# Five fetch buffers and a later place for two tiles' corner fetches in a four-layer convolution kernel

## The reference

```python
def _bilinear_sample_one(img, px, py):
    x0 = jnp.floor(px)
    y0 = jnp.floor(py)
    x1 = x0 + 1.0
    y1 = y0 + 1.0
    wx1 = px - x0
    wx0 = 1.0 - wx1
    wy1 = py - y0
    wy0 = 1.0 - wy1
    ...
    return tap(x0, y0, wx0 * wy0) + tap(x1, y0, wx1 * wy0) + tap(x0, y1, wx0 * wy1) + tap(x1, y1, wx1 * wy1)
...
x = x + _L0_conv_ref(_gn(x), L0_conv_Wg, L0_conv_bg, L0_conv_Wexp, L0_conv_bexp)
x = x + _L1_conv_ref(_gn(x), L1_conv_w_route, L1_conv_b_route, L1_conv_w_experts)
x = x + _L2_conv_ref(_gn(x), L2_conv_codebook)
x = x + _L3_conv_ref(_gn(x), L3_conv_w_grid, L3_conv_b_grid, L3_conv_w_conv)
return x
```

## Time and profile before

| what | value |
|---|---|
| median of three runs | 1796.74 us |
| the profiled execution | 1798.24 us |
| its span, first to last instruction | 1796.4 us |
| PE busy | 1571.3 us (87%) |
| DVE busy | 1501.9 us (84%) |
| POOL busy | 1220.5 us (68%) |
| ACT busy | 1105.4 us (62%) |

### The profile page before, as it was taken

One profiled execution on the slowest core, in us unless ns is written; L12 is line 12 of the kernel. 1 busy time (PEld: TensorE's weight loads), 2 busy tenths in 40 slices (PEclk: granted clock), 3 DMA queues, 4 the chain that ended last, 5 costly groups with the idle time before them and its releaser, 6 DMA issues.

```text
span 1796.4 us, 41875 instructions
## 1 busy us (share of the span) xinstructions
PE 1571.3 (87%) x15564; PEld 1294.5 (72%) x15564; DVE 1501.9 (84%) x2927; ACT 1105.4 (62%) x1547; POOL 1220.5 (68%) x1437
## 2 busy tenths in 40 slices
PE   4686689899998989889899899989998898988998
PEld 3545666688667876588667796678865797668998
DVE  5486589888998988878798788988899778987998
ACT  2021666477655866467665686648765676658996
POOL 6143467767778667685677867776777866778774
PEclk9898799999999999989998999999999999999999
DMA  7476965697768975599656997679776895335653
GB/s 163 118 174 133 212 193 165 178 238 215 195 177 199 237 207 162 158 225 209 195 161 166 242 218 196 172 191 240 221 194 165 211 224 166 84 90 162 164 155 86
DMA packets 280768, 326.09 MB, mean 182 GB/s; under 512 B 205572, under 2 KB 219924, under 8 KB 276720
## 3 DMA queue, kind: packets, MB, share of 16 engines
q1 hardware_dynamic: 235768, 226.01, 47.9%
q0 software_dynamic: 37040, 82.95, 19.7%
q10 hardware_dynamic: 7760, 14.45, 2.5%
HBM read 253.50 MB, written 56.40 MB: 173 GB/s over the span
## 4 chain that ended last, share of the span: by engine, by line
PE 38%; DVE 19%; DMA 13%; issue 8%; DVEq 7%; POOL 7%; SPq 5%; ACT 2%; ACTq 1%; POOLq 0%
PE bank L1444 22%; DMA words<-in_codebook,code 7%; DVE code L1311 5%; DVEq L1310 4%; POOL fetched L665 3%; PE bank L1526 3%; PE bank L1558 3%; POOL words L712 3%; SPq L472 2%; PE bank L1575 2%; DMA y_patches<-yc 2%; DVE strip L1078 2%; DVE samp L1098 2%; PE bank L1424 2%; DMA arena<-xp 1%
## 5 line engine op out<-in xcount | busy, mean ns | idle before, releaser
L665 POOL DMA_INDIRECT fetched<-row_pairs,corner x768 | 735.5, 958 | 360.6 <-issue 198.0
L1444 PE MATMUL bank<-lent,tent 128*128 128x160 f32 x6144 | 935.8, 307 | 16.9 <-ACT lent L845 11.6
L1444 PEld LDWEIGHTS bank<-lent,tent 128*128 128x128 f32 x6144 | 870.5, 195 | 104.0 <-issue 71.0
L831 ACT ACTIVATE tent<-lent,row_at_sb 128x768 f32<-128x768 f32 x512 | 448.9, 924 | 56.0 <-PE bank L1444 38.9
L835 ACT ACTIVATE tent<-tent 128x1536 f32<-128x1536 f32 x256 | 379.9, 1484 | 20.9 <-issue 0.4
L1078 DVE TENSOR_TENSOR strip<-bank,near 128x480 f32<-128x480 f32 x512 | 331.1, 648 | 67.2 <-PE bank L1444 61.1
L712 POOL DMA_INDIRECT words<-in_codebook,code x256 | 246.4, 963 | 104.1 <-issue 56.4
L1575 PE MATMUL bank<-cb,xs 64*128 64x512 f32 x512 | 217.8, 643 | 14.8 <-DVE code L1311 7.7
L1098 DVE TENSOR_REDUCE samp<-strip 128x192 f32<-128x960 f32 x186 | 214.5, 1153 | 15.2
L912 ACT COPY xs<-xn 32x128 f32<-32x128 f32 x256 | 75.5, 295 | 221.3 <-PE bank L1575 203.2
L820 ACT COPY samp_t<-bank 96x384 f32<-96x384 f32 x256 | 119.4, 467 | 129.2 <-PE bank L1431 54.7
(11 more groups left out here) (159 smaller groups left out, 1430.3 us busy)
## 6 DMA issues: line engine op xcount, KB each, us to landing
lent<-z_rows SPq DMA_DIRECT2D x254, 384.0 KB
picked_weights<-arena SPq DMA_DIRECT2D x12, 1800.0 KB
arena<-picked_weights SPq DMA_DIRECT2D x21, 720.0 KB
arena<-windows SPq DMA_DIRECT2D x276, 50.0 KB, 3.5
fetched<-row_pairs,corner POOLq DMA_INDIRECT x768
arena<-xp SPq DMA_DIRECT2D x90, 136.0 KB
arena<-row_pairs SPq DMA_DIRECT2D x64, 160.0 KB
slice<-picked_weights SPq DMA_DIRECT2D x14, 720.0 KB
```

Of the source, the lines that this page charges most:

```text
L665: pool.indirect_dma_start(fetched[:, N % FETCHES, k].rearrange("p q c -> p (q c)"), None, pairs_dram[b % 2], bass.IndirectOffsetOnAxis(ap= ...
L831: act.activation(w[:, piece], zs[:, N % SPREADS, :], ACT.Abs, bias=row_at[:, piece:piece + 1])
L1444: m = pe.matmul(STRIPS[j % 3][:, XW * C * e:XW * C * (e + 1)], tent[:, N % TENTS, c, DENSE * d + e], picture[:, b % 2, i, c], start=(c == ...
```

## The change

`fetched` gets five buffers in place of three, and a function `asked_by` says how many tiles' fetches are asked for when tile N's second half has passed. Outside scores a half then fetches five tiles ahead instead of three. At half 21, the first of scores, nothing is fetched, and at half 31 neither; so the fetches run four tiles ahead in the first half of scores and three tiles ahead in the second. At half 41 (spell) two tiles are fetched, at half 43 (norm3) one, at half 45 (rows) two, and then the distance is five again. Within a half with two tiles, the first fetch of each stands ahead of POOL's sum and the other four behind it. In front of the first half of all, 15 fetches are issued instead of 9. The number of fetches in all stays 768, and PE, DVE, ACT and SP keep their order.

```diff
--- before.py
+++ after.py
@@ -42,7 +42,7 @@
 FETCHED = TAPS - STRUNG
 TENTS = 3
 SPREADS = 4
-FETCHES = 3
+FETCHES = 5
 SHIFT = 14
 ZCUTS = 2
 CORNERS = 4
@@ -339,6 +339,20 @@
         for J in range(HALVES * ALL):
             POOL_SUMS.append(POOL_SUMS[-1] + added_by_pool(J))
 
+        def asked_by(N):
+            if N < 0:
+                return FETCHES
+            J = HALVES * N + 1
+            reached = (J + SHIFT) % (HALVES * GROUP_TILES) - SHIFT
+            if J < LEFT:
+                if PLACE["scores"][0] <= reached < PLACE["scores"][0] + SCORE_HALVES // 2:
+                    return N + FETCHES
+                if reached < PLACE["scores"][1] and reached >= PLACE["scores"][0]:
+                    return N + FETCHES - 1
+                if PLACE["spell"][0] <= reached < PLACE["norm3"][1]:
+                    return N + FETCHES
+            return N + 1 + FETCHES
+
         def by_pool(J):
             return POOL_SUMS[J + 1]
 
@@ -739,13 +753,14 @@
 
             def half(J):
                 N, d = divmod(J, HALVES)
-                if d == 1:
-                    fetch(N + FETCHES, 0)
+                asked = range(asked_by(N - 1), asked_by(N)) if d == 1 else range(0)
+                for M in asked:
+                    fetch(M, 0)
                 if J > 0 and added_by_pool(J - 1):
                     add_columns(J - 1)
-                if d == 1:
-                    fetch(N + FETCHES, 1)
-                    fetch(N + FETCHES, 2)
+                for M in asked:
+                    fetch(M, 1)
+                    fetch(M, 2)
 
             windows(0)
             for v in range(SLICES, NV):
```

## The result

The changed kernel takes 1826.45 us (median of seven runs, 1817.44 to 1845.48), the kernel before 1796.74 us in seven runs beside it. The ratio is 1.0158, with a 95% interval of 1.0125 to 1.0191: some 29 us slower. The forecast was 1827 us.

The account below looks back on a forecast made before the run. POOL's queue, last to arrive at the end of near in every group, was taken to hold PE. Added fetches + 52.5, scores - 16, last look-up - 6 gave + 30.5 us, forecast 1827 us; 8 times in 10, 1812 to 1847.

Parts of the forecast that it names:

- The added stretch: Spell to near: six more fetches delay POOL's last sum and so PE's turn of tile 24, 7.5 us per group.
- Its size: Spell to near, groups 1 to 7: 7 x 7.5 = 52.5 us added, counted in full.
- the prediction's own sign: The step on spell and near is wrong if last look-up to half 49's sum grows by less than 7 us.
- its other sign: Turn of tile 24 should still start about 0.1 us behind half 49's sum; well behind it means the step is wrong.
- Scores and the last look-up: Fetches leaving scores cut DVE's lost time by 16 us; the last look-ups come nearer DVE's codes, gaining 6 us.
- Fetch buffers: Fetches at longer distance wait for an older buffer, free earlier or equally so; costs and gains nothing.
- ACT behind the subtraction: Behind POOL's subtraction, 7.5 us later, ACT loses 4.9 us per group; no cost by itself.
- (first): Scores: words stay late because of busy DMA engines, so scores gain nothing; + 46.5 us, 1843 us; chance 0.13.
- (second): Turn of tile 24: POOL is not its releaser, so only gains remain; - 22 us, 1775 us; chance 0.06.
- (third): Row0 to norm2: PE's idle time gives back up to 32.6 us; 1795 us, no change; chance 0.08.
- The rule of the Trainium skill: POOL's fetch issue: by the rule six fetches hold POOL 0.3 us, some 2 us per run; the prediction rejected it.

Follow-up runs that it names:

- experiment 3: Changed kernel, but nothing left out in scores; two tiles still added behind the searches and left out in the following row0; 1834.22 us, ratio 1.0193 to the kernel before.
- experiment 6: Half the change: four buffers, one tile left out in scores and made up behind spell; 1807.86 us, ratio 1.0068 to the kernel before.
- second profile: Changed kernel run again without any edit, to profile it a second time; 1827.98 us, ratio 1.017 to the kernel before.
- experiment 1: Changed kernel with five buffers and fetches five tiles ahead everywhere, nothing left out or added; 1801.83 us, ratio 1.000 to the kernel before.
- experiment 5: Changed kernel's five buffers, but fetches three tiles ahead everywhere as before the change; 1789.43 us, ratio 0.9978 to the kernel before.
- experiment 4: Changed kernel with the sums of halves 47 and 49 made by DVE instead of POOL; 1809.63 us, ratio 1.0076 to the kernel before.
- experiment 7: Changed kernel, but two tiles left out behind spell and rows, made up in row0, none left out in scores; 1797.16 us, ratio 1.0005 to the kernel before.
- experiment 8: Changed kernel, but two tiles left out behind spell and rows, made up in pool and mix; 1794.04 us, ratio 0.9971 to the kernel before.
- experiment 10: Changed kernel with seven buffers, two tiles left out of scores and two behind the searches, made up in row stages; 1792.58 us, ratio 0.9957 to the kernel before.

## Why the prediction was right, step by step

*The added stretch.* The step that decides came out as worked out: POOL's later end is PE's later start. The turn of tile 24 starts 0.09 to 0.11 us behind the last sum in all seven groups, before and after. The new waits at the turns of tiles 20, 22 and 23 are 2.84 to 3.99, 0.79 to 2.12 and 2.19 to 4.96 us, where 2 to 3.5 were expected. At tile 22 five of the seven are shorter than that. Experiments 3 and 6 show the cost without the rest, and that it is proportional.

*Its size.* Forecast + 52.5 us, measured + 47.9: 6.84 us per group instead of 7.5. By the prediction's own sign, growth of less than 7 us, this step is narrowly missed in its size, while its other sign, the 0.1 us, held. The fetches did not become cheaper: over the seven groups, the 42 that were added took 56.3 us with the gaps ahead of fetches, 1.34 us each. POOL's other work in the stretch became shorter, above all the sums, by 7.9 us in all: in group 5 the nine sums' adds took 13.23 us instead of 14.72, and the subtraction 1.92 instead of 2.05. In the same stretch DVE's busy share fell from 34.41 of 41.0 us to 30.15 of 47.2 us. The two go together in the trace: in the changed kernel's second profile, 32 of POOL's 294 adds took over 0.12 us longer than the median of their line, all beside a DVE instruction, and none of the 77 adds during which DVE ran nothing did. No run here isolates it.

*Scores and the last look-up.* Forecast - 16 and - 6, measured - 13.3 and - 5.7. The waits moved as said: words 44.5 to 11.9 us (under 20 expected), DVE for scores 18.4 to 8.8 (under 8 expected, so this one narrowly missed), POOL waiting for codes 92.7 us.

*Fetch buffers.* Here the prediction had the wrong reason. Its step said that an older buffer "costs and gains nothing". This holds for a longer distance (experiment 1), but not for slack: in the second half of scores the changed kernel fetches three tiles ahead with five buffers, so that fetches hardly wait for the tile being weighed (from 8 us ahead of the first code to the last look-up 1.5 us in groups 1 to 7, 20.9 before), with look-ups queued behind them. In the front, slack alone gives 12.3 us of the 19.0 (experiment 5), and 12.1 beside the added stretch (experiment 3). The step on scores put the whole gain down to the tiles left out; in the changed kernel, leaving them out adds some 7 us to that. That is their share on top of slack. No run shows it alone, since every version here that leaves a tile out gives slack with it.

*ACT behind the subtraction.* Expected was a loss of 4.9 us per group; the new wait is 11.3 us in seven places, 1.6 us each. The likely reason, not shown, is that PE is held up at tile 20 already and what feeds ACT comes later with it. As the time goes by the turn of tile 24, this made no difference.

*The rivals.* Words did not stay late (first). POOL is the releaser (second): added time on POOL moved the turn one for one, and in experiment 4 the turn came free of POOL when its last sums were taken away. Nothing was given back in the row stages (third): 552.2 us against 551.9. The other direction of the third rival did show itself in experiments 7, 8 and 10: time won ahead of the turn is taken away there.

*What the prediction left out.* It has no term for PE's clock. PE's new waits went with a lower granted clock, 0.86 instead of 0.96 in group 5's stretch, and this used up PE's spare time ahead of the turn of tile 24. POOL's sum still came last there, by 0.06 us in group 7, so the forecast came out without the term.

*The number.* 1827 us against 1826.45 is closer than the terms behind it. The cost came out 4.6 us smaller than forecast and the gains together 3.0 us smaller, which nearly cancels, and most of the gain has a cause (slack) that the prediction had at nothing. That the total met so closely is luck; that POOL's queue decides it is not.

*The rule of the Trainium skill.* By the Trainium skill's "DMA: Bandwidth & Descriptors" (section "Anatomy of one DMA — SWDGE (gpsimd) path"), making the descriptors is a small part of a transfer's fixed cost. The six moved fetches lengthened POOL's stretch by 6.84 us per group here, where the estimate by the rule was 0.3 us. For this gather the trace disagrees with the rule, and the forecast that went by the row held.

## What to carry to other kernels

An engine that issues indirect DMAs is full although its busy share says 34 of 41 us, when a gap of 0.3 us stands between one issue and the next; count its steps, not its busy time, and look for a fixed 0.1 us between its last result and the start of a waiting engine, whatever releaser the profile names. Work can only be moved off a tight stretch into one where nobody waits for that engine: the same two tiles left out of scores gave a ratio of 0.9932 when they were made up in row0 and 1.0158 behind the searches. And a removed wait of 2 us is worth only as much as the distance to the next limit: here the time was lost again within 65 us.

## What was not expected of the hardware

After PE had stood idle for 3.99 us, the same 16 matmuls of 128x72 took 3.53 us at 1215.27, where they had taken 2.00 us, and four of the turn's took 1.06 us instead of 0.60. The granted clock of the whole stretch was 0.86 of 2.4 GHz instead of 0.96, and from 1214 to 1219 us it was 0.50, the lower of its two levels, 1.2 GHz. After the wait of 2.94 us at the turn of tile 23 it was low again. It cost no time at the turn of tile 24, since PE still came there ahead of POOL's sum, but by 0.06 to 0.76 us only in six of the seven groups.

The gap of 0.30 us stands between two indirect DMAs of POOL and not behind each: in the listing of the earlier trace rows the fetch that ends at 1194.70 + 0.94 = 1195.64 is followed by an add at 1195.66, and the next fetch starts 0.24 us behind the sum's last add. The step between two DMAs in a row has a median of 1.25 us in every kernel here, with 86 to 90% of the steps at 1.30 us or less and single ones up to 1.78. The prediction's count of 1.25 us per fetch holds all the same, since each fetch has one such gap ahead of it, 0.30 us behind a DMA and about 0.24 us behind an add.
